# A masked-attention layer on one core: both blocks' masks ahead of both blocks' scores, and GpSimd's LayerNorm 2 cut into six pieces

## The reference

```python
qkv = layer_norm(x, g1, be1) @ w_qkv              # 4096 x 384
scores = jnp.einsum('nhd,mhd->hnm', q, k) * SCALE
scores = jnp.where(adj != 0, scores, -jnp.inf)     # one 4096 x 4096 mask for all heads
attn = jax.nn.softmax(scores, axis=-1)
x = x + (attn @ v) @ w_proj + b_proj
h2 = layer_norm(x, g2, be2)
x = x + jax.nn.gelu(h2 @ w1 + b1) @ w2 + b2
```

## Time and profile before

| | |
|---|---|
| median of 3 runs | 1884.87 us (1881.31 to 1890.25) |
| the profiled execution | 1880.29 us |
| its span, first to last instruction | 1878.5 us |
| PE busy | 1723.5 us (92%) |
| DVE busy | 1412.5 us (75%) |
| ACT busy | 1301.7 us (69%) |
| POOL busy | 1177.6 us (63%) |
| granted PE clock, mean | 0.965 of full |

### The profile page before, as it was taken

One profiled execution on the slowest core, in us unless ns is written; L12 is line 12 of the kernel. 1 busy time (PEld: TensorE's weight loads), 2 busy tenths in 40 slices (PEclk: granted clock), 3 DMA queues, 4 the chain that ended last, 5 costly groups with the idle time before them and its releaser, 6 DMA issues. The chain is left out here.

```text
span 1878.5 us, 48359 instructions
## 1 busy us (share of the span) xinstructions
PE 1723.5 (92%) x17826; PEld 536.2 (29%) x17826; DVE 1412.5 (75%) x4495; ACT 1301.7 (69%) x1443; POOL 1177.6 (63%) x1113
## 2 busy tenths in 40 slices
PE   6999999899998999989998999989999899989985
PEld 3422222323222322323223232323223232222323
DVE  6878888777887788867887778867888678877600
ACT  4547777576776777667775867667776677757781
POOL 5934585567845787467855678457864678456441
PEclk9869999999999999999999999989999899999997
DMA  8710135002450035201360025300362024400000
GB/s 215 163 32 2 32 116 116 22 2 74 119 97 2 13 110 117 52 1 52 121 118 1 2 89 127 75 1 24 113 106 49 2 63 129 76 1 2 8 1 11
DMA packets 168847, 115.26 MB, mean 61 GB/s; under 512 B 139298, under 2 KB 149156, under 8 KB 168612
## 3 DMA queue, kind: packets, MB, share of 16 engines
q1 hardware_dynamic: 157860, 103.78, 22.8%
q10 hardware_dynamic: 10752, 8.39, 1.5%
HBM read 74.39 MB, written 4.19 MB: 42 GB/s over the span
## 5 line engine op out<-in xcount | busy, mean ns | idle before, releaser
L760 DVE CUSTOM_DVE_ANT_0 masked_out<-ring_ps,row_mask 128x512 bf16<-128x512 f32 x2048 | 1300.3, 687 | 253.3 <-PE ring_ps L957 215.5
L725 ACT ACTIVATE probs<-score_ps,score_scale 128x1024 f32<-128x1024 f32 x1024 | 1089.7, 1111 | 373.5 <-PE score_ps L1124 368.6
L517 POOL TENSOR_TENSOR probs<-probs,keep 128x1024 int32<-128x1024 int32 x256 | 604.5, 2361 | 329.8 <-ACT probs L725 320.3
L1020 PE MATMUL pv_ps<-probs,v_ones 128*17 128x512 f32 x4096 | 548.9, 609 | 33.4 <-POOL probs L517 33.4
L957 PE MATMUL ring_ps<-k_stack,q_stack 51*64 51x512 f16 x4096 | 512.3, 397 | 14.8 <-DVE row_max L760 10.2
L1124 PE MATMUL score_ps<-q_stack,k_stack 51*64 51x512 f16 x4096 | 427.7, 400 | 41.2 <-ACT probs L725 1.1
L1111 PE MATMUL score_ps<-mask_t,ident_bf 64*64 64x512 bf16 x3072 | 317.2, 393 | 30.2 <-ACT q_x L673 13.5
L957 PEld LDWEIGHTS ring_ps<-k_stack,q_stack 51*64 51x64 f16 x4096 | 167.8, 106 | 323.1 <-DVE row_max L760 147.3
L1124 PEld LDWEIGHTS score_ps<-q_stack,k_stack 51*64 51x64 f16 x4096 | 117.5, 104 | 357.0 <-PE score_ps L1111 347.4
L760 DVE DVE_READ_ACCUMULATOR2_ANT row_max<- 128x1 f32 x2048 | 169.8, 83 | 0.0
L1111 PEld LDWEIGHTS score_ps<-mask_t,ident_bf 64*64 64x64 bf16 x3072 | 92.1, 105 | 269.3 <-ACT probs L725 119.1
(11 more groups left out here) (106 smaller groups left out, 1002.3 us busy)
## 6 DMA issues: line engine op xcount, KB each, us to landing
adj_in<-adj SPq DMA_DIRECT2D x128, 512.0 KB, 3.9
xnT_dram<-attn ACTq DMA_DIRECT2D x8, 256.0 KB, 3.9
mask_t<-row_mask SPq DMA_TRANSPOSE x128, 3.3
xq<-xnT_dram ACTq DMA_DIRECT2D x8, 256.0 KB, 2.6
x_res<-x ACTq DMA_DIRECT2D x8, 256.0 KB, 4.4
out<-rows ACTq DMA_DIRECT2D x8, 256.0 KB, 2.6
w_sb<-L_gnn_w SPq DMA_DIRECT2D x2, 256.0 KB
probs<-x SPq DMA_DIRECT2D x1, 256.0 KB, 2.6
```

What stands on the lines that cost most here:

```text
L517: nc.gpsimd.tensor_tensor(view, view, keep[:, KEPT.index(m), :].unsqueeze(1).broadcast_to([128, 2, TILE]), ALU.mult).then_inc(probs_masked, 1)
L725: nc.scalar.activation(probs[:, (2 * g + n) % SLOTS, :], score_ps[:, half:half + 2, :].rearrange("p a n -> p (a n)"), ACT.Exp, scale=score ...
L760: nc.vector.tensor_tensor_reduce(out=masked_out[:, place % 3, :], in0=ring_ps[:, place % 3, :], in1=row_mask[:, j, ch * 512:(ch + 1) * 512 ...
L1020: last = nc.tensor.matmul(pv_ps[32 * k:32 * k + HD + 1, :], v_ones[:, block_of(g, b), 2 * p + a, :], probs[:, (2 * g + b) % SLOTS, a * TIL ...
```

## The change

1. PE, two-mask steps: the first two row units come first; then the masks of block 0, the masks of block 1, the scores of block 0, the scores of block 1. Before, the masks of block 0 stood ahead of the row units, and the masks of block 1 between the two scores. In pool steps the instructions keep their order; only the wait for the unmasked block's half of `score_ps` moves from ahead of the first two row units to behind them.
2. POOL: the work of `root2` is cut into six pieces (three Newton rounds, applies 0 and 1, applies 2 and 3, the addition), which stand in steps 12, 13, 14, 15, 16 and 18, each behind that step's `mask_probs`, where there is one.
3. What hangs on LayerNorm 2 moves back: `h2t` by one step (16, 17), `up` by two (19, 21, 23, 25), `down` by one (30 to 33), the output's store by one (34). The fills of q move to steps 31, 34, 37 and 41.

```diff
-UP_STEPS = [17 + 2 * f for f in range(FC)]
-ACT_FILLS = {15: ("h2t", 0), 16: ("h2t", 1), 28: ("q", 0), 32: ("q", 1), 35: ("q", 2), 40: ("q", 3)}
+UP_STEPS = [19 + 2 * f for f in range(FC)]
+ACT_FILLS = {16: ("h2t", 0), 17: ("h2t", 1), 31: ("q", 0), 34: ("q", 1), 37: ("q", 2), 41: ("q", 3)}
...
-DVE_FILLS.update({29 + s: ("down", s) for s in range(SUB)})
+DVE_FILLS.update({30 + s: ("down", s) for s in range(SUB)})
...
-APPLY_STEP = 12
-STORE_STEP = 33
+POOL_LN2 = [12, 13, 14, 15, 16, 18]
+STORE_STEP = 34
...
-            def root2(i):
+            def layer_norm2(i, k):
                 first = (i - 1) * ROOT_OPS
-                pool.wait_ge(ln2_step, (i - 1) * LN2_STEPS + LN2_STATS)
-                settled(pool)
-                for k in range(NEWTON):
-                    if k > 0:
+                if k < NEWTON:
+
+                    if k == 0:
+                        pool.wait_ge(ln2_step, (i - 1) * LN2_STEPS + LN2_STATS)
+                    else:
                         pool.wait_ge(root_step, first + 4 * k)
-                        settled(pool)
+                    settled(pool)
...
+                elif k < NEWTON + 2:
+                    pool.wait_ge(root_step, first + ROOT_OPS)
+                    settled(pool)
+                    for s in range(2 * (k - NEWTON), 2 * (k - NEWTON) + 2):
+                        nc.gpsimd.tensor_scalar(rows2[:, s, :], x_res[:, s, :], mean_var[:, s, 0:1], rstd[:, s:s + 1],
+                                                ALU.subtract, ALU.mult).then_inc(ln2_applied, 1)
+                else:
+
+                    pool.wait_ge(ln2_applied, (i - 1) * (SUB + 1) + SUB)
+                    settled(pool)
+                    nc.gpsimd.tensor_tensor(x_res[:, :, :], x_res[:, :, :],
+                                            b2_rows[:, :].unsqueeze(1).broadcast_to([128, SUB, DIM]), ALU.add)\
+                      .then_inc(ln2_applied, 1)
...
                 for g in range(STEPS):
-                    if d and g == APPLY_STEP:
-                        root2(i)
...
                     if c and g >= 1 and pool_step(g - 1):
                         mask_probs(i, bcd, g - 1)
+                    if d and g in POOL_LN2:
+                        layer_norm2(i, POOL_LN2.index(g))
...
                 for g in range(STEPS):
-                    if c:
-                        masks(g, 0)
                     for x in range(UNITS // 2):
                         row(g, x)
-                    if c:
+                    if c and pool_step(g):
                         scores(g, 0)
                         masks(g, 1)
+                        scores(g, 1)
+                    elif c:
+                        masks(g, 0)
+                        masks(g, 1)
+                        scores(g, 0)
                         scores(g, 1)
```

More of the change, by code:

```diff
@@ L734, in body @@
                     if d and g == STORE_STEP:
-                        act.wait_ge(row_taken, made(ROWS, i, bcd, DVE_PLACE[32]))
+                        act.wait_ge(row_taken, made(ROWS, i, bcd, DVE_PLACE[33]))
                         act.dma_start(tile_of(out_view, i - 1), rows2[:, :, :]).then_inc(out_stored, 16)
@@ L1104, in masks @@
                         pe.wait_ge(mask_in[m // PER_C], (i + 1) * (16 * SUB))
-                    if plain:
-                        return
                     upper, lower = slice(0, 64), slice(64, 128)
@@ L1117, in scores @@
                     p, m, even, odd, plain = block(g, n)
-                    if not plain:
+                    if plain:
+                        score_turn(i, bcd, SCORE_PLACE[g, n])
+                    else:
                         pe.wait_ge(masks_set, i * MASKED + masked_before(g, n) + 1)
```

## The result

| | before | after |
|---|---|---|
| median of the runs | 1883.1 us (4 runs, 1880.1 to 1890.3) | 1811.8 us (4 runs, 1806.8 to 1813.9) |
| ratio | | 0.9612, interval 0.9577 to 0.9647 |
| profiled execution, its span | 1880.3, 1878.5 us | 1812.5, 1810.7 us |
| mean granted clock of PE | 0.965 | 0.976 |
| steps of tiles 1 to 6, per tile | 217.4 us | 207.7 us |

The account below looks back on a forecast made before the run. PE's queue was taken to set the time. -10.5 per tile, -63 for six, -7.5 for tile 7 and -3 for tile 0 took 1880.3 to 1806.8; plus 3 gave 1810 us, range 1792 to 1838.

Parts of the forecast that it names:

- stall in steps 14, 15 and the clock behind it: Steps 14 and 15 take 6.2 us instead of 12.12, -5.9 per tile; half-level clock behind the stall goes, -1.6.
- plain pairs: Two-mask step plus pool step without other work: 5.54 to 5.43 us; thirteen per tile, -2.0.
- pairs 46 and 62, shift: Pairs with a shift fill outside steps 14 to 43: ACT's copy ends 0.24 us later, two pairs, +0.5 per tile.
- pairs with covered waits: Four pairs where PE work (sums, back, proj) covers the wait for ACT: each gains 0.05 to 0.24, -0.3 per tile.
- steps 16 to 43: Walked pair by pair with the moved ACT fills: 98.1 us against 99.4, -1.2 per tile.
- the rival with GpSimd late: GpSimd late by 1 to 2 us at masks 25, 27 or the second transposes: 1825 to 1845 us; chance 0.13.
- Only LayerNorm 2 pays: ACT's longer round trip eats all 0.24; pairs stay at 5.54, -7.5 per tile, about 1830 us; chance 0.18.
- PE gets all of it: ACT's end does not bind: 0.14 us more in some 200 pairs, 1783 us; chance 0.08.
- Weights of like rows don't overlap: Groups behind masks come after 0.52 us instead of 0.24; plain pair 6.0, about 1935 us; chance 0.03.
- The order does nothing: PE's drain stays, so the new order gains nothing; time close to about 1830 us; counted within a chance of 0.18.
- Tile 0 and the load ahead of it: Tile 0, which has no LayerNorm 2, was put at -3 us.
- Tile 7 and the tail: Tile 7, without q fills and ending without rows, masks 1 costing about +0.1 in ten pairs: -7.5 us.

Follow-up runs that it names:

- the kernels with short exponentials: Exponentials over 896 of 1024 columns (tile 0's first four steps whole), in the changed kernel and the kernel before: 1789.5 us and 1875.6 us, one run each.
- the pieces alone: Changed kernel with PE's loop and waits of before; GpSimd's six LayerNorm 2 pieces and the moved fills stay: 1829.7 us, ratio 0.9709.
- the order alone: Kernel before with only PE's loop and its wait for score_ps changed; LayerNorm 2 and fills stay: 1859.3 us, ratio 0.9873.
- the kernel with the wait: Changed kernel where GpSimd, in step 12, waits for DVE's LayerNorm 2 statistics before the mask of step 11: 1809.5 us, one run.
- masks 0 ahead in step 12: Changed kernel with GpSimd's wait in step 12, a third row unit behind pool-step masks, and step 12's masks 0 before its rows: 1802.9 us, ratio 0.9597.

## Why the prediction was right, step by step

Forecast for the profiled execution 1806.8 us, measured 1812.5: -73.5 against -67.8. Per tile, as an average over tiles 1 to 6 (the table of the experiments has medians):

| step of the prediction | forecast | measured | from |
|---|---|---|---|
| stall in steps 14, 15 and the clock behind it | -5.9 -1.6 | -6.9 | pair 14, 13.16 to 6.22 |
| plain pairs | -2.0 | -1.0 | without pair 12: -1.5 |
| pairs 46 and 62, shift | +0.5 | +0.5 | 5.96 and 6.01 to 6.22 |
| pairs with covered waits | -0.3 | -0.5 | pairs 4, 6, 52 |
| steps 16 to 43 | -1.2 | -1.7 | 99.69 to 98.01 |
| sum | -10.5 | -9.75 | stretches of tiles 1 to 6 |

The -1.6 was the excess of the average tile over tile 4. Of it 1.0 lay in pair 14 itself (13.16 on average, 12.12 in tile 4) and 0.3 in steps 16 to 43; without the stall it is gone, as forecast (207.70 on average, 207.66 in tile 4). The walk through steps 16 to 43 gave 98.1 for tile 4, where 97.94 was measured. So the first and the fifth row belong together: -8.7 forecast, -8.6 measured.

**Right, with its mechanism.** The stall: GpSimd's masks reach PE in time at all places but one (0.4 us, in the tail, where the kernel before has the same wait), so the rival with GpSimd late fell. It was close: where 0.3 us of slack was walked, the masks of step 25 end 0.07 to 0.08 before PE's values begin, and those of step 27 0.22 to 0.24, in one tile 0.05. Where PE did wait for a mask before (step 11), it began 0.05 to 0.06 behind its end, so at step 25 next to nothing was left. The order: gaps of 0.24 between rows, masks, masks and q and k; values at 1.67; exponentials at +1.23; a wait of 0.29 for ACT ahead of the pool step's masks, where 0.32 was forecast. The two halves of the change run alone give its two terms, and the kernels with short exponentials show the new wait to be ACT's.

**The rivals.** *Only LayerNorm 2 pays* is what the pieces alone measured (1829.7, where 1830 was worked out); the order's 0.11 per pair is real. *PE gets all of it* could not have happened: without ACT's wait the pair stops at 5.31 by DVE's chain, and the 0.14 more per pair that this rival priced would have been 0.11 at best. *Weights of like rows don't overlap* fell by the plain pair's timeline: two groups of masks that lie in the same four quarters follow at 0.24 (the line with x8 begins 0.47 before the next group). The Trainium skill (TensorE: Matmul & The Clock Gate, Part 3) says that weight loads overlap running matmuls only where the row group differs; this case's trace disagrees. *The order does nothing* fell by the same gaps and by the order alone, 24.5 us.

**Mis-sized: the plain pairs.** -2.0 was forecast and -1.0 came. 0.6 of the missing 1.0 is pair 12, which was walked at -0.1 like its neighbours and came at +0.51. The step costed GpSimd's pieces "at nothing" after asking only whether GpSimd is in time for PE. It did not ask what the mask's `keep`, which moved from behind LayerNorm 2 to the moment when DVE ends its part, does to DVE (0.30, shown by the kernel with the wait), and it took rows first to be harmless where DVE is late (0.21, shown by masks 0 ahead in step 12). The rest is in the count: thirteen plain pairs, two with a shift and four covered make nineteen, but only seventeen lie outside steps 14 to 43. Twelve are plain and three covered, if pair 10, with DVE's statistics in it, counts as plain; it gained only 0.06. And the pairs that had gained by DVE's chain, 2, 8, 50 and 58, are four and not five.

**Mis-sized: the ends of the run.** Tile 0 and the load ahead of it gave 4.1 where 3 was forecast (tile 1 begins at 317.44 instead of 321.51; in the other kernels of this study it began between 311 and 325, so this term is mostly scatter, and that it makes up for half of what tile 7 lacks is luck). Tile 7 and the tail gave 5.3 where 7.5 was forecast. The steps are not short of it: from the start of tile 7 to the start of its last pair (step 62) it is 199.8 before and 191.7 after, -8.1. The tail gave 2.8 back. The second half of the projection of the last tile, before and then after:

```profile
1842.48 2.05 PE L1068 MATMUL ring_ps<-wp_pad,attn 128*128 128x128 f32 x16 [0.52 <-DVE x_res L866]
```

```profile
1772.63 3.78 PE L1071 MATMUL ring_ps<-wp_pad,attn 128*128 128x128 f32 x16 [0.52 <-DVE x_res L869]
```

and the stretches around them (reciprocals and the first half, then the second half), before and then after:

```profile
1835.20:1842.40 7.20, 5.46 (x56) 4.99 (x56) 1.30 (x3) 0.00 (x0) 0.00 (x0) 0.76 0.01 2
1842.40:1844.60 2.20, 2.05 (x16) 1.86 (x16) 0.06 (x2) 0.00 (x0) 0.00 (x0) 1.00 0.00 0
```

```profile
1764.68:1772.60 7.92, 6.16 (x56) 5.38 (x56) 1.32 (x3) 0.00 (x0) 0.00 (x0) 0.63 0.01 2
1772.60:1776.40 3.80, 3.77 (x16) 3.49 (x16) 0.00 (x0) 0.00 (x0) 0.00 (x0) 0.50 0.00 0
```

The same 16 matmuls ran at 2.4 GHz before and at 1.2 GHz after, behind the same short waits of PE (0.80, 0.39 and 0.89 us for ACT and DVE). From the first of these stretches to the end of the projection this makes 2.4 us of the 2.8. The order alone and the pieces alone had 2.05 in this line, but tails no shorter: there the output's last matmuls ran at the half level (1.78 to 2.08 a group instead of 1.16). What decides which part of the tail gets which level is open; no term of the sum had a place for it.

**Small ones.** The pairs with sums and back gained 0.23 each, the upper end of the 0.05 to 0.24 put down for them: their wait is covered, and the whole 0.24 of PE's queue shows. Of the nine late pairs of tile 7 from 44 to 60, which run without rows, eight cost 0.10 to 0.12 each (4.98 to 5.09 in the plain ones), as forecast; pair 54 costs nothing.

## What to carry to other kernels

A gain in one engine's queue is cut off by the next loop around it: add up each engine's round trip through the new order before pricing it, and look for the second floor behind the first. When a long piece of work is cut up and other operations slip ahead of it, ask not only whether they are in time, but what runs beside them at their new place, and on which other engine. Between dependent groups of small matmuls any one group fills the gap, but half a group costs as much as a whole one.

## What the runs showed of the hardware

- A VectorE operation on 128x4 int32 with one input took 0.47 us instead of 0.17 when it began during GpSimd's 0.62 us `tensor_scalar`, and ended 0.02 after it; made to run at another time it took 0.17 in all eight places. The VectorE operation just ahead, on 128x4 float32, had begun 0.03 us before the `keep` and took 0.17. The Trainium skill (SBUF — State Buffer, SBUF: two separate sides) says that the two engines share a pair of ports, which the one that starts first holds for its whole instruction, where VectorE's is in a two-port mode or has two inputs in SBUF. The trace agrees with such a hold; whether this VectorE operation, with its one input, ran in a two-port mode no run here shows.
- q and k, which wait by semaphore for the masks of their own bank to finish, begin 0.46 to 0.47 behind the first of them, where a group without such a wait begins 0.24 behind the one ahead; with another group of masks in between, which takes 0.24, no wait is left. Two matmuls of a group of four cost the same 0.24, and 0.31 ahead of the values.
- A stall of PE of up to 5.0 us costs more than itself. With the pieces alone pair 14 got 7.1 shorter on average. The stall (4.4 to 5.0 us) is 4.7 of that and the `h2t` fill, which left step 15, 0.4 (in tile 4 its matmuls begin at 1030.94 and the next step at 1031.30); by an estimate from these figures some 2 us are left, in matmuls that ran behind the stall at less than the full clock (0.69 to 0.86 over the pair, 2.05 us at the full level for what takes 3.78 at the half in the tail). In the kernel with the order alone, which keeps it, the clock granted in steps 14 and 15 of tile 4 was 0.72, and the pair stands at 12.32; in the changed kernel it is 1.00 there:

```profile
1005.42:1017.74 12.32, 7.52 (x71) 1.96 (x68) 5.52 (x17) 5.17 (x7) 10.85 (x10) 0.72 0.00 0
```
